# A four-layer network as a software pipeline: engine orders from a list scheduler, and elementwise steps moved between engines

## Time and profile before

| | us |
|---|---|
| median of 3 runs | 2094.04 (2093.27 to 2095.57) |
| the profiled execution | 2099.33 |
| its span, first to last instruction | 2097.5 |
| TensorE busy | 1651.5 (79%) |
| VectorE busy | 1770.0 (84%) |
| ScalarE busy | 1035.9 (49%) |
| GpSimd busy | 913.8 (44%) |

### The profile page before, as it was taken

How to read it: one execution, slowest core, us unless ns; L and a number is a source line. 1 busy time by engine, 2 the same in 40 slices (tenths; PEclk the granted TensorE clock), 3 DMA queues, 4 the chain that set the end, 5 groups by cost and what they waited for, 6 DMA issues and landing times. The chain is left out here.

```text
span 2097.5 us, 22567 instructions
## 1 busy us (share of the span) xinstructions
PE 1651.5 (79%) x5875; PEld 725.3 (35%) x5948; DVE 1770.0 (84%) x3142; ACT 1035.9 (49%) x1745; POOL 913.8 (44%) x676
## 2 busy tenths in 40 slices
PE   3375577778996889868997799878997899779856
PEld 1122123232452335322452335332452335234324
DVE  6577899989879998979989998999989987987830
ACT  3247444825555454735556355734547344734312
POOL 0101534454437434554346434464346544665510
PEclk9977699979997999979997899979997899999978
DMA  4100222222222222222231222222222223223300
GB/s 108 46 0 21 72 79 89 92 69 77 75 92 65 85 71 86 85 67 78 74 101 65 81 76 76 96 75 72 76 96 71 76 85 106 86 99 113 110 10 11
DMA packets 94601, 157.95 MB, mean 75 GB/s; under 512 B 10940, under 2 KB 23660, under 8 KB 94468
## 3 DMA queue, kind: packets, MB, share of 16 engines
q1 hardware_dynamic: 94468, 156.43, 22.9%
HBM read 143.83 MB, written 12.58 MB: 75 GB/s over the span
## 5 line engine op out<-in xcount | busy, mean ns | idle before, releaser
L1226 POOL TENSOR_TENSOR prod<-state,c_all 128x512 f32<-128x512 f32 x512 | 669.6, 1312 | 706.8 <-DVE state L1203 644.0
L1203 DVE TENSOR_TENSOR_SCAN state<-decay,ps_b 128x512 f32<-128x512 f32 x512 | 619.7, 1210 | 9.7 <-issue 0.4
L750 PE MATMUL ps_y<-prod,idf 128*128 128x512 f32 x1024 | 610.6, 689 | 4.8 <-DVE u L1216 3.6
L1210 DVE TENSOR_TENSOR ps_b<-du,ps_b 128x512 f32<-128x512 f32 x512 | 347.7, 679 | 87.3 <-PE ps_b L743 86.8
L919 ACT ACTIVATE decay<-delta,a_neg 128x512 f32<-128x512 f32 x512 | 359.3, 719 | 32.3 <-DVE state L1203 29.3
L743 PE MATMUL ps_b<-b_rows,sel_b 48*128 48x512 bf16 x512 | 209.9, 411 | 155.0 <-DVE state L1203 152.7
L750 PEld LDWEIGHTS ps_y<-prod,idf 128*128 128x128 f32 x1024 | 183.8, 207 | 136.3 <-issue 109.9
L743 PEld LDWEIGHTS ps_b<-b_rows,sel_b 48*128 48x128 bf16 x512 | 47.8, 94 | 467.3 <-DVE state L1203 332.5
L619 PE MATMUL ps_x<-xT,w 128*128 128x512 bf16 (+1 forms) x391 | 132.0, 422 | 80.1 <-DVE arena_l L1095 65.6
L826 ACT ACTIVATE arena_l<-ps_x 128x512 f32<-128x512 f32 (+1 forms) x104 | 61.8, 594 | 190.8 <-PE ps_x L619 189.7
L535 PE MATMUL ps_x<-hT,win 128*128 128x512 bf16 (+1 forms) x455 | 135.6, 441 | 21.4 <-DVE arena_b L1171 16.6
(11 more groups left out here) (230 smaller groups left out, 2422.2 us busy)
## 6 DMA issues: line engine op xcount, KB each, us to landing
c_all<-c_rows SPq DMA_DIRECT2D x512, 256.0 KB
c_rows<-arena_l SPq DMA_DIRECT2D x32, 256.0 KB
out<-arena_b SPq DMA_DIRECT2D x8, 512.0 KB
x_in<-in_base SPq DMA_DIRECT2D x8, 256.0 KB
c_all<-in_winT SPq DMA_DIRECT2D x1, 1280.0 KB, 7.5
arena_b<-in_w_fc SPq DMA_DIRECT2D x1, 1024.0 KB, 5.7
arena_b<-in_w_proj SPq DMA_DIRECT2D x1, 1024.0 KB, 5.0
w<-in_w1T SPq DMA_DIRECT2D x1, 792.0 KB, 5.9
```

Of the source, the lines that this page charges most:

```text
L750: nc.tensor.matmul(ps_y[:], idf[:], prod[:, n % NP, :], start=(n % NST == 0), stop=(n % NST == NST - 1)).then_inc(reduced, 1)
L1203: nc.vector.tensor_tensor_scan(state[:, n % NS, :], decay[:, n % NDA, :], ps_b[:, n % NDB, :], 0.0, ALU.mult, ALU.add).then_inc(scanned, 1)
L1210: nc.vector.tensor_tensor(ps_b[:, j % NDB, :], du[:, slot(s, ct), :], ps_b[:, j % NDB, :], ALU.mult).then_inc(driven, 1)
L1226: nc.gpsimd.tensor_tensor(prod[:, n % NP, :], state[:, n % NS, :], c_all[:, n % NC, :], ALU.mult).then_inc(multiplied, 1)
```

## The change

In `iteration`, slots give way to `weave`: a list scheduler, run when the program is built, that plays the scan and the chains on five engines with fixed durations (`BUSY`, `SCAN_BUSY`, in units near 10 ns), a handover of 12 units between dependent steps, and one port that GpSimd's steps and VectorE's steps outside the list `APART` share. At each choice the engine that can start first takes the offer with the greatest urgency: the weight from `URGENT` (eight numbers per chain, by position) times the work that the chain has left. The order that comes out is what each engine runs. `alone` and `together` are as before, with changed weights in `COST`.

Steps move: `shift`, `probs`, `v_relu`, `wo_relu`, `round`, `eps16` from VectorE to ScalarE (`shift` as maximum minus x, the exponential then with scale -1); `d_round` becomes `d_one` and `d_less` on ScalarE; `d_fix`, `d_sum` and `gated_y` go from VectorE to GpSimd. The gate's intermediate tiles move from SBUF into the unused part of its PSUM bank, with one copy more (`gate_twin`). Waits follow the steps. The core of the diff, cut:

```diff
-    r = [[("V", (site, "stats"))], [("V", (site, "aggr"))], [("V", (site, "round"))], [("V", (site, "eps16"))],
+    r = [[("V", (site, "stats"))], [("V", (site, "aggr"))], [("A", (site, "round"))], [("A", (site, "eps16"))],
...
-    steps = [(0, "V", "v_bias"), (1, "V", "v_relu")]
+    steps = [(0, "V", "v_bias"), (1, "A", "v_relu")]
...
-                  (b + 6, "V", ("shift", i)), (b + 7, "A", ("exp", i)), (b + 8, "V", ("sum", i)),
-                  (b + 9, "V", ("recip", i)), (b + 10, "V", ("probs", i)),
+                  (b + 6, "A", ("shift", i)), (b + 7, "A", ("exp", i)), (b + 8, "V", ("sum", i)),
+                  (b + 9, "V", ("recip", i)), (b + 10, "A", ("probs", i)),
...
-        steps += [(k, "P", ("d", i)), (k + 1, "A", ("d_abs", i)), (k + 2, "A", ("d_exp", i)), (k + 3, "A", ("d_log", i)),
-                  (k + 5, "V", ("d_sum", i)), (k + 3, "V", ("d_round", i)), (k + 4, "V", ("d_fix", i)),
-                  (k + 6, "G", ("delta", i)), (k + 7, "G", ("du", i))]
+        steps += [(k, "P", ("d", i)), (k + 1, "A", ("d_abs", i)), (k + 2, "A", ("d_exp", i)), (k + 3, "A", ("d_one", i)),
+                  (k + 4, "A", ("d_less", i)), (k + 5, "A", ("d_log", i)), (k + 5, "G", ("d_fix", i)), (k + 6, "G", ("d_sum", i)),
+                  (k + 7, "G", ("delta", i)), (k + 8, "G", ("du", i))]
...
-            r[-3].append(("V", ("gated_y", i - 1)))
+            r[-3].append(("G", ("gated_y", i - 1)))
...
+BUSY = {
...
+    "G": {"add": 225, "rms": 98, "rstd": 98, "root": 98, "gate_root": 541, "delta": 122, "du": 122, "d_fix": 122, "d_sum": 122, "gated_y": 122},
...
+SCAN_BUSY = {"decay": 62, "spread": 33, "drive": 60, "scan": 114, "product": 125, "sum": 87, "taken": 66, "load": 6}
+HANDOVER = 12
...
+CROSS = {("early", "y_turned"): ("late", ("up3", MCH - 1)), ("early", "cw_turned"): ("late", ("weigh", MCH - 1)),
+         ("late", ("m", "add")): ("back", ("w", "add")), ("late", ("x_tanh", 0)): ("back", ("wout", 1))}
+for i in range(1, MCH):
+    CROSS[("late", ("up3", i))] = ("late", ("gated", i - 1))
+for ct in range(CT - 1):
+    CROSS[("back", ("gated_y", ct))] = ("taken", ct)
+    CROSS[("late", ("d_abs", ct))] = ("taken", ct)
...
+URGENT = {"late": (0.32, 0.21, 0.17, 1.42, 0.34, 0.61, 0.01, 0.02),
+          "early": (10.39, 34.83, 6.82, 0.21, 3.35, 1.44, 0.16, 15.73),
+          "back": (17.26, 1.18, 330.85, 0.1, 0.06, 9.73, 0.79, 0.05),
+          "scan": (1.15, 30.65, 1781.42, 14, 0.66, 0.61, 1.19, 2.87)}
...
+class Chain:
+    def __init__(self, rounds, urgent):
+        self.rounds, self.at, self.ready = rounds, 0, 0
+        self.left = [sum(1 for _ in rnd) for rnd in rounds]
+        self.begun = [{e: 0 for e in "PAVGS"} for _ in rounds]
+        self.steps = [{e: [st for st in rnd if st[2] == e] for e in "PAVGS"} for rnd in rounds]
+        length = [max(sum(busy(e, st[0], st[3]) for st in by[e]) for e in "PAVGS") + HANDOVER for by in self.steps]
+        self.rest = [urgent[k * 8 // len(length)] * sum(length[k:]) for k in range(len(length))] + [0]
+        self.end = 0
+    def head(self, e):
+        if self.at >= len(self.rounds):
+            return None
+        k = self.begun[self.at][e]
+        return self.steps[self.at][e][k] if k < len(self.steps[self.at][e]) else None
+    def take(self, e, until):
+        self.begun[self.at][e] += 1
+        self.left[self.at] -= 1
+        self.end = max(self.end, until)
+        while self.at < len(self.rounds) and self.left[self.at] == 0:
+            self.at += 1
+            self.ready = self.end + HANDOVER
...
+def weave(chains, steps):
+    scan = {e: [(j, part) for j in steps for part in range(3) if scan_entries(e, j, part)] for e in "PAVGS"}
+    own = {(op, n) for e in scan for j, part in scan[e] for op, n, _ in scan_entries(e, j, part)}
+    own |= {(st[0], st[3]) for chain in chains for rnd in chain.rounds for st in rnd}
+    at = {e: 0 for e in "PAVGS"}
+    free = {e: 0 for e in "PAVGS"}
+    port = {"V": 0, "G": 0}
+    done, order = {}, {e: [] for e in "PAVGS"}
+    def ready_at(deps):
+        deps = [d for d in deps if d in own]
+        return None if any(d not in done for d in deps) else max([0] + [done[d] + HANDOVER for d in deps])
+    for _ in range(sum(len(v) for v in scan.values()) + sum(sum(chain.left) for chain in chains)):
+        best = None
+        for e in "PAVGS":
+            offers = []
+            if at[e] < len(scan[e]):
+                j, part = scan[e][at[e]]
+                entries = scan_entries(e, j, part)
+                here = [(op, n) for op, n, _ in entries]
+                when = ready_at([d for _, _, deps in entries for d in deps if d not in here])
+                if when is not None:
+                    held = port["V"] if e == "G" else 0
+                    offers.append((max(free[e], when, held), -URGENT["scan"][(j - steps[0]) * 8 // len(steps)] * (steps[-1] + 1 - j), None, None))
+            for chain in chains:
+                st = chain.head(e)
+                if st is not None:
+                    cross = CROSS.get((st[0], st[3]))
+                    when = ready_at([cross] if cross is not None else [])
+                    if when is not None:
+                        held = port["G"] if e == "V" and name_of(st[3]) not in APART else port["V"] if e == "G" else 0
+                        offers.append((max(free[e], when, chain.ready, held), -chain.rest[chain.at], chain, st))
+            if offers:
+                first = min(o[0] for o in offers)
+                mine = min((o for o in offers if o[0] <= first + 1), key=lambda o: o[1])
+                if best is None or mine[0] < best[0][0]:
+                    best = (mine, e)
+        (when, _, chain, st), e = best
+        if chain is None:
+            j, part = scan[e][at[e]]
+            at[e] += 1
+            for op, n, _ in scan_entries(e, j, part):
+                when += SCAN_BUSY[op]
+                done[(op, n)] = when
+            order[e].append(("scan", j, part))
+        else:
+            when += busy(e, st[0], st[3])
+            chain.take(e, when)
+            done[(st[0], st[3])] = when
+            order[e].append(st)
+        if e == "G" or e == "V" and chain is not None and name_of(st[3]) not in APART:
+            port[e] = when
+        free[e] = max(free[e], when)
+    return order, max(free.values())
...
+        g_q, g_c, g_s, g_tw, g_rk, cw, cwr = (
+            ps_x[:, XE, n * NT * NEXP:(n + 1) * NT * NEXP].rearrange("p (t e) -> p t e", t=NT) for n in range(1, 8))
+        g_eq = ps_x[:, XE, 256:512].rearrange("p (t i j) -> p t i j", t=NT, i=NEXP)
...
+            elif name == "shift":
+                eng.wait_ge(early["V"], ea(s, "V", ("max", i)))
+                for j in range(2):
+                    ins = act(ee[:, i % 2, j, :], ee[:, i % 2, j, :], ACT.Identity, bias=mx[:, i, j:j + 1], scale=-1.0)
+            elif name == "probs":
+                eng.wait_ge(early["V"], ea(s, "V", ("recip", i)))
+                for j in range(2):
+                    ins = act(ee[:, i % 2, j, :], ee[:, i % 2, j, :], ACT.Copy, scale=er[:, i, j:j + 1])
+            elif name in ("v_relu", "wo_relu"):
+                eng.wait_ge(early["V"], ea(s, "V", "v_bias" if name == "v_relu" else "wo_bias"))
+                dst = (vv if name == "v_relu" else yo).rearrange("p t d -> p (t d)")
+                ins = act(dst, dst, ACT.Relu)
+            elif i == "round":
+                eng.wait_ge(early["V"], ea(s, "V", (name, "aggr")))
+                nc.scalar.copy(mb[name][:], mv[name][:, :, 0])
+                ins = nc.scalar.copy(vb[name][:], mv[name][:, :, 1])
+            elif i == "eps16":
+                eng.wait_ge(early["A"], ea(s, "A", (name, "round")))
+                ins = act(vb[name][:], vb[name][:], ACT.Identity, bias=eps[:])
...
+            elif name == "d_one":
+                eng.wait_ge(late["A"], la(s, "A", ("d_exp", i)))
+                if i >= 2:
+                    eng.wait_ge(late["G"], la(s, "G", ("d_sum", i - 2)))
+                ins = act(d_q[:, i % 2, :], d_t(i), ACT.Identity, bias=1.0)
+            elif name == "d_less":
+                eng.wait_ge(late["A"], la(s, "A", ("d_one", i)))
+                ins = act(d_q[:, i % 2, :], d_q[:, i % 2, :], ACT.Identity, bias=minus[:])
...
+            elif name == "gate_twin":
+                own("gate_bias")
+                ins = nc.vector.tensor_copy(g_tw, g_bi[:])
             elif name in ("gate_gt", "gate_eq"):
-                own("gate_bias")
-                sj = g_bi[:].rearrange("p t (o j) -> p t o j", o=1).broadcast_to([P, NT, NEXP, NEXP])
+                own("gate_twin")
+                sj = g_tw.rearrange("p t (o j) -> p t o j", o=1).broadcast_to([P, NT, NEXP, NEXP])
...
+            elif name == "d_fix":
+                eng.wait_ge(late["A"], la(s, "A", ("d_less", i)))
+                ins = tt(d_q[:, i % 2, :], d_t(i), d_q[:, i % 2, :], ALU.subtract)
+            elif name == "d_sum":
```

(52 more changed lines are left out.)

124 lines of the change are left out of this document (59 added, 65 removed), and 2 rows, old and new, of the table b.

## The result

The median is 1948.06 us (1944.15 to 1955.81, four runs), against 2094.48 for the kernel before on the same chip: a ratio of 0.9306, interval 0.9276 to 0.9336. The forecast was 1874, in a range of 1800 to 1955. Direction and range held; the point was 74 us too low. The range held by little and not by its main case: the forecast's own, A, ran from 1845 to 1935, and 1948 lies inside only because the range also took in C (1954). The profiled execution took 1944.15, its span 1942.4, with a granted clock of 0.92 in the mean.

What follows compares the result with a forecast made beforehand. VectorE, 91.2% busy in the middle iterations, was taken as the main bound. Savings of 170 (five middle), 33, 18 and 5, less 5 for filling and 1 for draining, gave -220: 1879.3 profiled, 1874 us median, range 1800 to 1955.

Steps and rivals of the forecast that it cites:

- A: Whole kernel: VectorE stays the bound at about today's share, 1874 us, own range 1845 to 1935; chance 0.56.
- C: Middle iterations: TensorE becomes the bound, its 201.5 us at 93% making 217 an iteration, 1954 in total; chance 0.14.
- VectorE's work and the moved steps: Middle iteration: moves take 33.7 us off VectorE's 217.1, leaving 186.0 with 2.6 of added waiting.
- growth of waiting by 2.6: VectorE's remaining instructions, middle iteration: held up 2.6 us more as GpSimd's share grows from 48% to 65%; bounds 0 to 7.2.
- with today's 91.2% the iteration is 204: Middle iterations: VectorE's 186.0 us at an unchanged busy share gives 204, 34 less each, 170 over five.
- I let the two cancel: Middle iterations: better mixing by the list is set against more handovers and TensorE's 201.5 us, net nothing.
- Rival D: GpSimd's queue: late products stop the scan, VectorE stands 2.5 us seven times, 17 an iteration, 1979 in total; chance 0.07.
- four groups of 5.9 us: GpSimd's softplus steps (d_fix, d_sum, delta, du): three scan steps of 3.7 us cover each, given a product between groups.
- a decay queued behind: ScalarE: decays delayed behind the moved steps, priced at nothing, or 5 us if the four buffers' cover is gone.
- B: Middle iterations: heavy VectorE stretches lie over heavy TensorE ones, share 96.5%, 193 us an iteration, 1804 in total; chance 0.16.
- E: Iteration's end: the list leaves one chain's rest to run alone, 45 us, 249 an iteration, 2150 in total; chance 0.06.
- The rule on two-input work on GpSimd: Twelve GpSimd steps: by bare prices they give back 8.1 us, not 16.5, total some 45 us higher.

Runs made afterwards that it cites:

- order_refit: The kernel before with the list scheduler, every step on its old engine and urgencies searched anew for that placing: 1973.47 us, ratio 0.9408 to the kernel before.
- moves_only: The changed kernel with the slots of the kernel before instead of the list scheduler, all moves kept: 2134.17 us, ratio 1.0169 to the kernel before.
- proj_twice: The changed kernel with the ternary block's projection matmuls run twice on TensorE, order the same: 2060.0 us, ratio 0.9827 to the kernel before.
- tail_light: The changed kernel with GpSimd's d_fix and d_sum on 4 of 512 columns, order the same: 1928.74 us, ratio 0.9205 to the kernel before.
- flat_urgency: The changed kernel with all 32 urgencies of the list scheduler set to 1: 2124.88 us, ratio 1.0145 to the kernel before.
- softmax_v: The changed kernel with shift and probs back on VectorE, list order worked out anew with the same urgencies: 2016.09 us, ratio 0.9608 to the kernel before.

## Why the prediction was right or wrong

**VectorE's work and the moved steps: right.** The middle groups of after (as the earlier trace rows); VectorE:

```profile
L1378 DVE TENSOR_TENSOR_SCAN state<-decay,ps_b 128x512 f32<-128x512 f32 x320 | 388.4, 1214 | 32.3 <-ACT decay L1121 20.4 <-DVE ps_b L1385 0.4
L1385 DVE TENSOR_TENSOR ps_b<-du,ps_b 128x512 f32<-128x512 f32 x320 | 218.2, 682 | 36.3 <-PE ps_b L917 36.1
...
L1171 DVE TENSOR_SCALAR arena_e<-arena_e 128x1024 bf16<-128x1024 bf16 x20 | 12.0, 602 | 4.0 <-ACT arena_e L951 4.0
...
L1262 DVE TENSOR_TENSOR x<-x,xn 128x1024 bf16<-128x1024 bf16 x5 | 8.8, 1759 | 0.0
...
L1183 DVE TENSOR_SCALAR ps_x<-g 128x32 f32<-128x32 f32 x5 | 0.9, 189 | 0.0
```

ScalarE:

```profile
L959 ACT ACTIVATE arena_e<-arena_e,er 128x512 bf16<-128x512 bf16 x40 | 26.9, 731 | 1.0 <-DVE er L1180 1.0
L955 ACT ACTIVATE arena_e<-arena_e,mx 128x512 bf16<-128x512 bf16 x40 | 26.8, 724 | 23.2 <-DVE mx L1174 23.2
L974 ACT ACTIVATE arena_e<-arena_e 128x512 bf16<-128x512 bf16 x40 | 24.8, 626 | 0.0
L1070 ACT ACTIVATE arena_l<-arena_l,minus 128x512 f32<-128x512 f32 x20 | 14.4, 718 | 0.0
L1067 ACT ACTIVATE arena_l<-arena_l 128x512 f32<-128x512 f32 x20 | 12.9, 644 | 0.1
```

GpSimd:

```profile
L1401 POOL TENSOR_TENSOR prod<-state,c_all 128x512 f32<-128x512 f32 x320 | 408.1, 1281 | 331.9 <-DVE state L1378 270.7 <-PE ps_y L924 58.8 <-DVE g L1193 1.4
L1434 POOL TENSOR_TENSOR du<-delta,u 128x512 f32<-128x512 f32 x20 | 25.5, 1275 | 1.0 <-POOL delta L1430 0.9
L1423 POOL TENSOR_TENSOR arena_l<-arena_l 128x512 f32<-128x512 f32 x20 | 25.4, 1272 | 0.0
L1450 POOL TENSOR_TENSOR u<-u,arena_b 128x512 f32<-128x512 f32 x20 | 25.4, 1270 | 5.0 <-issue 5.0
```

Over the whole span VectorE has 1521.5 us (1564 was said), ScalarE 1198.9 (1186), GpSimd 1000.3 (1056). More than half of VectorE's difference is the filling, which the forecast left out of this sum: there it fell from 151.5 to 128.7. Shift and probs take 0.72 and 0.73 us, not 0.62. (The 146 us of ScalarE that the prediction calls "even doubled" are the sum undoubled, 127.4 + 18.7; doubled it is 165. Measured are 147.9 of 210.8, so nothing hung on it.) The gate's L1183, for L997, takes 0.19: as said.

**The growth of waiting by 2.6: wrong in sign, small.** With the two-input steps gone from VectorE, GpSimd's own fell from 1472 to 1275 ns, its product from 1323 to 1281, and the scale from 630 to 602. Both sides hold each other up less. Twelve steps at 1.47 were 17.7 an iteration; they are 12 x 1.27 = 15.3.

**The step that failed: "with today's 91.2% the iteration is 204", and "I let the two cancel".** The share fell to 87.3%, which at 184.1 us is 210.8: 34 of the 65 us. The price of the moves' handovers and of a fuller TensorE was not offset by the better order; how it divides between these two was not measured. order_refit and moves_only show both sides singly: the order raised the share to 94.9% without the moves, and the moves in slots brought it down to 78.3%. Of the cases the one that came nearest is C, 1954, whose mechanism (TensorE) proj_twice shows for the stretches where it is full. C alone isn't the whole of it: VectorE's added time still cost four fifths, and TensorE's 91.1% stands beside VectorE's 87.3%. TensorE's busy time did shrink as said (201.5 to 192.1, clock 0.91 to 0.95), but by less than VectorE's. A sum of the two stretches would have pointed there before: where the earlier trace rows have TensorE at 19.57 of 20 and VectorE at 13.11, work taken from VectorE can give little.

**Rival D, GpSimd late: in part, at an iteration's end.** The seventh iteration was forecast at 190.4 and took 205.9; in tail_light, with 10.3 us less on GpSimd, it is 10.9 shorter, 2.9 of them by TensorE's clock at its start (above). I had priced four groups of 5.9 us as covered by products between them. At the iteration's end they aren't, because the work of the other chains that would cover them is done. At the end of the seventh, products stand behind softplus's steps and VectorE stands 8.6 us until it can take y (in tail_light 4.4):

```profile
1684.28 1.26 POOL L1401 TENSOR_TENSOR prod<-state,c_all 128x512 f32<-128x512 f32 x1
1685.50 1.26 POOL L1430 TENSOR_TENSOR delta<-du,delta 128x512 f32<-128x512 f32 x1
1686.73 1.25 POOL L1427 TENSOR_TENSOR du<-du,arena_l 128x512 f32<-128x512 f32 x1
1687.95 1.25 POOL L1401 TENSOR_TENSOR prod<-state,c_all 128x512 f32<-128x512 f32 x1
...
1691.45 0.75 DVE L1391 SCALAR_TENSOR_TENSOR u<-u,dpar,ps_y 128x512 f32<-128x512 f32 x1 [8.56 <-PE ps_y L924]
```

What D said of the scan, that it stands for a product, is in no wait of after's middle or seventh. The timeline of after at 828 shows the scan waiting for a decay instead:

```profile
824.07 1.28 ACT L1073 ACT_TABLE_LOAD   x1
...
826.53 1.28 ACT L1062 ACT_TABLE_LOAD   x1
...
828.37 0.71 ACT L1121 ACTIVATE decay<-delta,a_neg 128x512 f32<-128x512 f32 x1
828.98 0.71 ACT L1070 ACTIVATE arena_l<-arena_l,minus 128x512 f32<-128x512 f32 x1
829.11 1.22 DVE L1378 TENSOR_TENSOR_SCAN state<-decay,ps_b 128x512 f32<-128x512 f32 x1 [2.28 <-ACT decay L1121]
```

So "a decay queued behind", priced at nothing or 5 us if the cover is gone, is real: the scan waited 20.4 us for decays in five iterations, 4 an iteration. What stands before this decay is softplus's ScalarE work, and with it two loads of the function table, 1.28 us each. Neither forecast nor scheduler has them as a price that depends on the order: after has ten in a middle iteration, before eight.

**Rivals B and E.** B (1804) needed 96.5%; even without the moves the best order got 94.9%. E (2150, one chain's rest alone at the end) didn't come in after. Its direction did in flat_urgency, 2124.88: the order lives by its urgencies, as was said there. Its mechanism isn't shown: in the third iteration of flat_urgency VectorE's emptiest 20 us lie in the middle (783 to 803, 8.36 busy), and not at the end.

**Edges.** The filling grew by 11.4 us, 5 were said. In softmax_v it is 233.7 against after's 239.8, so shift and probs cost 6.1 (4.3 said); the other 5.3 come with the rest of the change and were not tried singly. The first iteration took 192.3 for 188, the eighth 161.9 for 153. The eighth has VectorE at 79.5% where it had 86.4%, and got 3.8 us longer; proj_twice added 13.4 to it, so the projection is on the path there as well. The draining is 3.1 us shorter, where 1 more was said; it varies as much among kernels with the same draining (88.2 to 93.2), so nothing is read from it.

**The rule on two-input work on GpSimd** ("GPSIMD Engine Reference", 4.1, of the Trainium skill) would have had the total 45 us higher than the forecast, 1919. The trace agrees with its speed: 1270 ns on GpSimd, 672 bare on VectorE. What the moves gained on a fitted order, one point, is nearer to what it makes one expect than my 16.5 us an iteration: all moves together took 23.4 us off VectorE between order_refit's middle iteration and after's, and gave 7.9. The runs can't single the GpSimd steps out, since the softplus and softmax moves weren't separated on orders that are each known to be good.

## What to carry to other kernels

Where several chains share in-order queues, measure the order and the placement apart: here the order brought six points and the placement one, and the placement alone made the kernel slower. Don't carry the busy share of the leading engine over to a lighter one; ask per stretch who is full, since where another engine stands at 19.6 of 20 the saved work can give little. Priorities fitted to one set of steps are part of that set: change a step's engine and the comparison also measures the lost fit.

## What the runs showed of the hardware

An instruction's price depends on the neighbour in both directions. GpSimd's two-input step of 512 f32 columns takes 1472 ns in the mean beside the old VectorE work and 1275 beside the new; VectorE's addition to x (L1262), 658 ns at the least before, takes 1758 at the median after, in the same shape. Which of the two is longer goes with which starts first:

```profile
546.22 1.63 POOL L1401 TENSOR_TENSOR prod<-state,c_all 128x512 f32<-128x512 f32 x1 [0.69 <-DVE state L1378]
546.64 1.76 DVE L1262 TENSOR_TENSOR x<-x,xn 128x1024 bf16<-128x1024 bf16 x1
```

After, each of the five long additions starts 0.33 to 0.42 us after a product of GpSimd; before, in seven of eight, the product starts 0.16 to 0.25 us after the addition, the addition takes 0.66 to 0.67 and the product 1.54 to 1.64. The start times were not changed singly.

On ScalarE, 512 columns take 626 ns in the exponential and 644 in `d_one`, but 718, 724 and 731 in the three instructions with a per-partition operand (`minus`, `mx`, `er`): 74 to 105 ns for that operand. The Trainium skill, "ScalarE: Activation LUTs", What ACT_TABLE_LOAD costs, has about 93 ns for each such operand; the trace agrees.
